# Unread identity products on TensorE in a two-layer decoder: first group's front and last group's FFN

## The chip, the cores and the metric

The kernel runs on one core of a Trainium2 chip. The metric is the device time in microseconds (us) of one execution, the median of several runs. TensorE multiplies at one of two clock levels, 1.2 or 2.4 GHz. The profile gives the level as the granted clock, a share of full speed (0.50 or 1.00; a mean of both where a stretch holds a change).

## What is computed

The reference passes x of shape (16, 128, 256) through two decoder layers, in float32:

```python
x = layernorm(x + L0_attn(x))          # causal attention, one head
x = layernorm(x + L0_xattn(x, ctx))    # 16 heads of 8 channels, causal convolution with k
x = layernorm(x + L0_ffn(x))           # ternary weights, quantised inputs
x = layernorm(x + L1_attn(x))          # linear recurrence with a decay
x = layernorm(x + L1_xattn(x, ctx))    # 16 query heads, 4 key heads of 128
x = layernorm(x + L1_ffn(x))           # fp8 gate and up, gelu, fp8 down
```

The 16 sequences are independent of each other until the end.

## The kernel before

Two sequences make a group, so there are eight groups. The work of a group goes through stations. Station "a" holds the front (`front`: layer 0's attention and its convolution) and, three groups later, the last FFN (`ffn`); "c" holds the ternary FFN and the recurrence; "q", "x", "y" and "o" hold the second cross attention; "s" is the set-up of the weights. Each engine has its own list of steps of these stations, interleaved by a written-out string of letters (`ORDER`), and runs it strictly in that order. Semaphores join the engines. PSUM has eight banks: A0 and A1 for station a, C0 and C1 for c, E0 and E1 for the scores, EQ for queries and keys, EY for the output product.

Before there is other work, TensorE has only the first group and the set-up: at the start it waits on VectorE, ScalarE and GpSimd between short bursts. At the end nothing is left but the last group's FFN: the last nine letters of TensorE's order are nine steps of station a.

The first group's front, in TensorE's order, with the lines of the profile:

- L972 scores (`a_sc`), then L978 transposes of the probabilities (`a_pT`), which wait for VectorE's normalised S0, then L983 `a_y`, which waits for ScalarE's copy PT0.
- L933 `abs_ps`, a sum for the ternary weights, which waits for ScalarE's L438 and so for a load of weights. VectorE makes the mean from it (L604 to L606), after it has written X of the front; ScalarE's two tanh (L443) wait for the mean, and stand in ScalarE's order ahead of its copy XTA (L477).
- L944 transposes X (`b_xT`), L991 `b_skip`, then eight convolution steps u0 to u7 (L1007, L1009, L1010), which wait for the products `prod` that VectorE and GpSimd make from XTA (L232). GpSimd's next products wait for u1.
- L1016 `b_oT`, then L1123, the first keys of the cross attention, which waits for the last load of the set-up, and L938, which waits for ScalarE's decay table.

The last group's FFN: L944 transposes X once the cross attention's norm is out (`ne_out`); L1037 makes the gate and up halves in four steps (`f_gf`), each of which waits until ScalarE and VectorE have emptied A0 and A1; then a table load and the gelu on ScalarE (L492), a product on VectorE (L719), L1044 transposes, ScalarE's copies A8T (L497), and L1051, the down product.

Of the kernel before, what the change touches and what calls it, by code (L numbers as in the profile page):

```python
# [6 lines left out]
P = 128  # L7
HALVES = DIM // P
GB = 2
GROUPS = BATCH // GB  # L10
# [5 lines left out]
XHEADS, XKV, XDIM = 16, 4, 128  # L16
# [9 lines left out]
def build_decoder(nc, a):  # L26
# [4 lines left out]
    with ctx:  # L31
        def sb(name, shape, dt=F):
            return ctx.enter_context(nc.sbuf_tensor(name, [P] + list(shape), dt))

        def sem(name):
            return ctx.enter_context(nc.semaphore(name))
# [16 lines left out]
        ident_bf = sb("ident_bf", [P], BF)  # L53
# [76 lines left out]
        A0, A1, C0, C1, E0, E1, EQ, EY = bank  # L130
        EB = (E0, E1)

        def rows(t):
            return t[:].rearrange("p (b d) -> p b d", b=GB)

        def cols(t):
            return t[:].rearrange("p (k r) -> p k r", k=HALVES)
# [7 lines left out]
        def seq(b):  # L145
            return slice(b * P, (b + 1) * P)
# [14 lines left out]
        sems = {n: sem(n) for n in names}  # L161

        def sig(ins, name):
            return ins.then_inc(sems[name], 1)

        def nth(g, per=1, j=0):

            return g * per + j + 1

        def settled(eng):  # L170
            eng.sem_inc(sems["passed"], 1)
# [19 lines left out]
        def a_free(eng, kind, g):  # L191

            if kind == "front" and g >= AHEAD:
                eng.wait_ge(sems["nf_out"], nth(g - AHEAD))
            elif kind == "front" and g > 0:
                eng.wait_ge(sems["na_out"], nth(g - 1, 3, 2))
            elif kind == "ffn":
                eng.wait_ge(sems["na_out"], nth(min(g + AHEAD - 1, GROUPS - 1), 3, 2))
                if g > GROUPS - AHEAD:
                    eng.wait_ge(sems["nf_out"], nth(g - 1))  # L200
# [702 lines left out]
        def _(pe):  # L903
# [37 lines left out]
            def transpose_rows(src, dst, name):  # L941
                for b in range(GB):
                    for k in range(HALVES):
                        ins = nc.tensor.transpose(cols(dst)[:, k, seq(b)], src[:, b, k * P:(k + 1) * P], ident[:])  # L944
                sig(ins, name)

            def project_rows(dst, xt, w, name):
                for b in range(GB):
                    for k in range(HALVES):
                        ins = nc.tensor.matmul(rows(dst)[:, b], xt(k, b), w(k), start=k == 0, stop=k == HALVES - 1)  # L950
                sig(ins, name)

            def front(g):
                x = X[g % XBUF]
                yield
                pe.wait_ge(sems["loaded_a"], 16 * for_group["a"])
                pe.wait_ge(sems["na_out"], nth(g, 3, 0))
                transpose_rows(Z, A0, "a_zT")
                yield
                pe.wait_ge(sems["a_xn"], nth(g))  # L960
                pe.wait_ge(sems["w_qk_in"], 1)
                for e in range(HALVES):
                    for k in range(HALVES):
                        ins = nc.tensor.matmul(cols(A1)[:, e], w_qk[:, k, e * P:(e + 1) * P], XTA[:, k], start=k == 0, stop=k == HALVES - 1)
                sig(ins, "a_qv")
                pe.wait_ge(sems["w_vo_in"], 1)
                project_rows(A0, lambda k, b: XTA[:, k, seq(b)], lambda k: w_vo[:, k], "a_qv")
                yield
                pe.wait_ge(sems["a_q"], nth(g))
                for b in range(GB):  # L970
                    for k in range(HALVES):
                        ins = nc.tensor.matmul(A1[:, seq(b)], QT[:, k, seq(b)], XTA[:, k, seq(b)], start=k == 0, stop=k == HALVES - 1)  # L972
                sig(ins, "a_sc")
                yield
                pe.wait_ge(sems["a_v"], nth(g))
                pe.wait_ge(sems["a_p"], nth(g))
                for b in range(GB):
                    ins = nc.tensor.transpose(A0[:, seq(b)], S0[:, seq(b)], ident[:])  # L978
                sig(ins, "a_pT")
                yield  # L980
                pe.wait_ge(sems["a_pTc"], nth(g))
                for b in range(GB):
                    ins = nc.tensor.matmul(rows(A1)[:, b], PT0[:, seq(b)], V[:, b], start=True, stop=True)  # L983
                sig(ins, "a_y")
                yield
                pe.wait_ge(sems["na_out"], nth(g, 3, 1))
                transpose_rows(x, A0, "b_xT")
                yield
                pe.wait_ge(sems["pool_const"], 2)
                pe.wait_ge(sems["b_w"], nth(g))  # L990
                sig(nc.tensor.matmul(A1[:], skip_w[:], SK[:].rearrange("p b d -> p (b d)"), start=True, stop=True), "b_skip")  # L991
                for u in range(8):
                    yield
                    hq, lb = u // 2, u % 2
                    if hq == 0:
                        pe.wait_ge(sems["b_kv0"], nth(g))
                    else:
                        pe.wait_ge(sems["b_kv"], nth(g, 3, hq - 1))
                    if u == 1:
                        pe.wait_ge(sems["b_skc"], nth(g))  # L1000
                    if u >= 2:
                        pe.wait_ge(sems["b_z"], nth(g, 8, u - 2))
                    out = (A0, A1)[u % 2][:].rearrange("p (b h n) -> p b h n", b=GB, h=4)
                    for h in range(4):
                        mv_ = prod[:, hq % 2, :, :, h * 64:(h + 1) * 64]
                        if lb == 0:
                            ins = nc.tensor.matmul(out[:, :, h], taps[:, hq * 4 + h, 0:P], mv_[:, 0], start=True, stop=True)  # L1007
                        else:
                            nc.tensor.matmul(out[:, :, h], taps[:, hq * 4 + h, 0:P], mv_[:, 1], start=True, stop=False)  # L1009
                            ins = nc.tensor.matmul(out[:, :, h], taps[:, hq * 4 + h, P:], mv_[:, 0], start=False, stop=True)  # L1010
                    sig(ins, "b_yps")
                yield
                pe.wait_ge(sems["b_ot"], nth(g))
                for b in range(GB):
                    for k in range(HALVES):
                        ins = nc.tensor.transpose(rows(A0)[:, b, k * P:(k + 1) * P], OT[:, k, b], ident[:])  # L1016
                sig(ins, "b_oT")

            def ffn(g):
                yield  # L1020
                a_free(pe, "ffn", g)
                pe.wait_ge(sems["ne_out"], nth(g))
                transpose_rows(X[g % XBUF], A0, "f_xT")
                for j in range(2 * GB):
                    yield
                    b, nh = j // 2, j % 2
                    if j == 0:
                        pe.wait_ge(sems["stage_used0"], 6)
                        pe.wait_ge(sems["stage_used1"], 6)
                    pe.wait_ge(sems["f_x8"], nth(g))  # L1030
                    if j >= 1:
                        pe.wait_ge(sems["f_g16"], nth(g, 2 * GB, j - 1))
                        pe.wait_ge(sems["f_f16"], nth(g, 2 * GB, j - 1))
                    settled(pe)
                    for k in range(2):
                        for h in range(HALVES):
                            ins = nc.tensor.matmul((A0, A1)[k][:], X8[:, h, seq(b)], w_gf[:, k, h, nh * BANK:(nh + 1) * BANK],  # L1037
                                                   start=h == 0, stop=h == HALVES - 1)
                    sig(ins, "f_gf")
                for b in range(GB):  # L1040
                    yield
                    pe.wait_ge(sems["f_a"], nth(g, GB, b))
                    for k in range(FFN_K):
                        ins = nc.tensor.transpose(as_bf((A0, A1)[b])[:, seq(k)], G16[:, b, seq(k)], ident_bf[:])  # L1044
                    sig(ins, "f_aT")
                for b in range(GB):
                    yield
                    pe.wait_ge(sems["f_a8"], nth(g, GB, b))
                    settled(pe)
                    for k in range(FFN_K):  # L1050
                        ins = nc.tensor.matmul((A0, A1)[b][:, 0:DIM], A8T[:, b, k], w_ln[:, k], start=k == 0, stop=k == FFN_K - 1)  # L1051
                    sig(ins, "f_y")
# [265 lines left out]
```

## Time and profile before

| | |
|---|---|
| median of 3 runs | 937.77 us (936.29 to 937.84) |
| profiled execution, its time | 936.48 us |
| its span, first to last instruction | 934.7 us |
| around the span | 1.8 us |
| mean granted clock of TensorE | 0.958 |
| TensorE busy | 829.3 us (89%) |
| VectorE busy | 714.5 us (76%) |
| ScalarE busy | 500.4 us (54%) |
| GpSimd busy | 263.0 us (28%) |

A busy share counts from an instruction's start to its modelled end; matmuls overlap, so it says when TensorE had work, not how fast it worked. The granted clock says that.

### The profile page before, as it was taken

The page shows a single profiled execution, that of the slowest core. Times are in us where ns is not written, and L with a number is a line of the kernel's source. Part 1 is how long each engine was busy: PE and PEld are TensorE (multiplying, and loading weights), DVE is VectorE, ACT ScalarE, POOL GpSimd, SP SyncE. Part 2 cuts the span into 40 slices and gives each one's busy share as a digit, 9 for nine tenths or more (in the row PEclk, how much of TensorE's full clock was granted, in tenths as well). Part 3 has the DMA queues.
Part 4 walks back from the last instruction along what each step waited for, and adds up shares of the span by engine and source line. Part 5 has one row for each costly group of instructions (what it writes and reads, how often), then busy time and mean ns, then how long its engine had stood idle before and what let it go on. Part 6 is the DMA issues. An engine that isn't in the chain of part 4 may idle for free.

```text
span 934.7 us, 14078 instructions
## 1 busy us (share of the span) xinstructions
PE 829.3 (89%) x4858; PEld 636.6 (68%) x4874; DVE 714.5 (76%) x1735; ACT 500.4 (54%) x1283; POOL 263.0 (28%) x298
## 2 busy tenths in 40 slices
PE   5654868998999999999999999998999999999964
PEld 4533746787686767976779768876779677767742
DVE  3587887878798889787988879688989696756443
ACT  3354116615544773368553587419552767577833
POOL 0323511343333133423134311442143311231100
PEclk9577989999999999999999999999999999999985
DMA  8861010000001000010000000010000000000000
GB/s 276 291 208 55 1 24 12 12 10 14 19 5 24 1 12 23 2 23 1 13 23 18 7 8 17 13 23 1 24 1 1 1 12 1 1 13 12 1 12 11
DMA packets 37062, 28.64 MB, mean 31 GB/s; under 512 B 18688, under 2 KB 34560, under 8 KB 36608
## 3 DMA queue, kind: packets, MB, share of 16 engines
q1 hardware_dynamic: 36992, 27.74, 9.8%
q8 instruction: 39, 0.64, 0.3%
q14 instruction: 31, 0.25, 0.1%
HBM read 25.64 MB, written 2.10 MB: 30 GB/s over the span
## 4 chain that ended last, share of the span: by engine, by line
PE 47%; DVE 34%; issue 10%; ACT 7%; POOL 1%; DMA 1%; SPq 1%; DVEq 0%; POOLq 0%; ACTq 0%
PE bank L1130 7%; PE bank L1226 6%; PE bank L950 5%; DVE S L879 4%; PE bank L1215 3%; PE bank L1205 3%; PE bank L1007 2%; PE bank L1123 2%; PE bank L1009 2%; PE bank L1010 2%; DVE amax L767 2%; PE bank L1037 2%; DVE H L766 2%; DVE mx L882 2%; DVE X L641 2%
## 5 line engine op out<-in xcount | busy, mean ns | idle before, releaser
L1130 PE MATMUL bank<-XTE,w_xq 128*128 128x256 f32 x512 | 126.1, 390 | 7.4 <-ACT QA L542 4.2
L575 ACT ACTIVATE S<-S,mx 128x128 f32<-128x128 f32 x256 | 99.4, 393 | 46.1 <-DVE mx L882 45.6
L1226 PE MATMUL bank<-w_xo,OX 128*128 128x256 f32 x512 | 116.2, 380 | 1.6 <-ACT OX L584 1.6
L1130 PEld LDWEIGHTS bank<-XTE,w_xq 128*128 128x128 f32 x512 | 96.5, 194 | 27.9 <-ACT QA L542 8.4
L1226 PEld LDWEIGHTS bank<-w_xo,OX 128*128 128x128 f32 x512 | 95.6, 190 | 18.2 <-issue 4.5
L541 ACT ACTIVATE QS<-bank,per_partition_sb 128x256 f32<-128x256 f32 x128 | 60.4, 472 | 80.9 <-PE bank L1130 80.8
L333 POOL TENSOR_TENSOR rq<-vq,minus_half 128x8 f32<-128x8 f32 x32 | 53.8, 1682 | 158.8 <-DVE vq L852 158.7
L879 DVE SCALAR_TENSOR_TENSOR S<-bank,rq,xmask 128x128 f32<-128x128 f32 x256 | 71.8, 343 | 15.4 <-PE bank L1205 10.5
L232 POOL TENSOR_TENSOR prod<-XTA,ccolA 128x256 f32<-128x256 f32 x96 | 63.0, 686 | 38.4 <-PE bank L1010 31.2
L1205 PEld LDWEIGHTS bank<-KTX,QA 128*128 128x128 f32 x512 | 63.5, 191 | 10.8 <-issue 9.3
L584 ACT ACTIVATE OX<-bank,bv_sb 128x512 f32<-128x512 f32 x64 | 43.6, 689 | 50.6 <-PE bank L1215 28.2
L1205 PE MATMUL bank<-KTX,QA 128*128 128x128 f32 x512 | 68.2, 278 | 0.7 <-ACT OX L584 0.6
L1215 PE MATMUL bank<-PT,VX 128*128 128x512 f32 x128 | 65.9, 606 | 1.8 <-ACT PT L579 1.7
L1123 PE MATMUL bank<-w_xkv_sb,ccolE 128*128 128x512 f32 x128 | 61.1, 600 | 1.0 <-DVE KX L857 0.9
L542 ACT ACTIVATE QA<-bank,per_partition_sb 128x256 f32<-128x256 f32 x128 | 60.7, 474 | 0.0
L1009 PE MATMUL bank<-prod,taps_sb 128*128 128x128 f32 x256 | 51.4, 283 | 1.2 <-DVE Zc L692 0.9
L579 ACT ACTIVATE PT<-bank 128x512 f32<-128x512 f32 x64 | 37.7, 600 | 26.5 <-PE bank L1210 26.4
L692 DVE TENSOR_TENSOR Zc<-bank,ccolA 128x512 f32<-128x512 f32 x64 | 43.7, 683 | 9.6 <-PE bank L1010 5.8
L1010 PE MATMUL bank<-prod,taps_sb 128*128 128x128 f32 x256 | 50.5, 280 | 0.0
L575 ACT ACTIVATION_READ_ACCUMULATOR S<-S,mx 128x1 f32 x256 | 48.9, 191 | 0.0
L886 DVE TENSOR_TENSOR S<-S,rs 128x512 f32<-128x512 f32 x64 | 46.3, 723 | 2.2
L1210 PE MATMUL bank<-ident,S 128*128 128x128 f32 x256 | 38.9, 277 | 9.0 <-DVE S L886 8.9
(222 smaller groups left out, 1780.8 us busy)
## 6 DMA issues: line engine op xcount, KB each, us to landing
xin<-in_x SPq DMA_DIRECT2D x8, 256.0 KB, 2.6
taps_sb<-in_taps SPq DMA_DIRECT2D x1, 2048.0 KB, 11.1
cnat<-in_ctx SPq DMA_DIRECT2D x8, 256.0 KB, 2.8
ccolA<-in_ctxT SPq DMA_DIRECT2D x32, 64.0 KB, 2.7
ccolE<-in_ctxT SPq DMA_DIRECT2D x16, 128.0 KB, 2.2
w_xq<-in_L_xattn_Wq SPq DMA_DIRECT2D x1, 2048.0 KB, 12.0
w_xo<-in_L_xattn_Wo SPq DMA_DIRECT2D x1, 2048.0 KB, 16.8
out_x<-X SPq DMA_DIRECT2D x8, 256.0 KB, 2.1
```

The lines of the kernel that those rows point to most:

```text
L232: ins = eng.tensor_tensor(prod[:, hq % 2, k, b].rearrange("p (h j i) -> p h j i", i=CONV_CH, j=CONV_CH), v.unsqueeze(2).broadcast_to([P, 4 ...
L541: nc.scalar.activation(QS[:, h], q, ACT.Square, bias=bq[:, hh:hh + 1])
L542: ins = nc.scalar.activation(QA[:, n % 2, h], q, ACT.Identity, bias=bq[:, hh:hh + 1])
L575: ins = nc.scalar.activation(S[:, b, seq(h)], S[:, b, seq(h)], ACT.Exp, bias=mx[:, b, h:h + 1], accum_out=sm[:, b, h:h + 1])
L879: ins = nc.vector.scalar_tensor_tensor(s3[:, h], EB[b][:, seq(h)], rq[:, n % 2, b * XGROUP + h:b * XGROUP + h + 1], xmask[:], ALU.mult, AL ...
L1009: nc.tensor.matmul(out[:, :, h], taps[:, hq * 4 + h, 0:P], mv_[:, 1], start=True, stop=False)
L1010: ins = nc.tensor.matmul(out[:, :, h], taps[:, hq * 4 + h, P:], mv_[:, 0], start=False, stop=True)
L1123: ins = nc.tensor.matmul(EQ[:], ccolE[:, k, b], w_xkv[:, k, v], start=k == 0, stop=k == HALVES - 1)
L1130: ins = nc.tensor.matmul(cols(EQ)[:, h], w_xq[:, k, hh * XDIM:(hh + 1) * XDIM], XTE[:, k], start=k == 0, stop=k == HALVES - 1)
L1205: ins = nc.tensor.matmul(EB[b][:, seq(h)], QA[:, n % 2, h, seq(b)], KTX[:, b, n], start=True, stop=True)
L1215: sig(nc.tensor.matmul(EB[b][:], VX[:, b, n * XDIM:(n + 1) * XDIM], PT[:, b], start=True, stop=True), f"e_o{b}")
L1226: ins = nc.tensor.matmul(rows(EY)[:, b], OX[:, h, b], w_xo[:, n * XGROUP + h], start=n == 0 and h == 0 and b == 0, stop=n == XKV - 1 and h ...
```

## The change

A helper issues n products of the bf16 identity with itself (128 by 128 by 128) into a bank that is free at the time. Nothing reads them, and they signal nothing. They stand behind the signalling instruction of a step, so no signal of the step itself is moved, and ahead of the next step's wait. In the first group there are 24, 30, 24 and 80 of them; in the last group's FFN 56 ahead of its first transposes, 10 after each of the first three `f_gf` steps and 50 after the fourth. Two waits are new on TensorE: for `pool_const` at 2 (GpSimd has made ident_bf and skip_w), and for the last `e_vq` (VectorE has read EQ for the last time).

```diff
+            def keep_clock(spare, n):
+
+                for _ in range(n):
+                    nc.tensor.matmul(spare[:, 0:P], ident_bf[:], ident_bf[:], start=True, stop=True)
@@ front, behind a_sc
+                if g == 0:
+                    pe.wait_ge(sems["pool_const"], 2)
+                    keep_clock(EY, 24)
@@ front, behind a_y
+                if g == 0:
+                    keep_clock(EY, 30)
@@ front, behind b_skip
+                if g == 0:
+                    keep_clock(EY, 24)
@@ front, behind b_oT
+                if g == 0:
+                    keep_clock(EY, 80)
@@ ffn
-                yield
+                last = g == GROUPS - 1
+                yield
+                if last:
+                    pe.wait_ge(sems["e_vq"], nth(g, XKV, XKV - 1))
+                    keep_clock(EQ, 56)
                 a_free(pe, "ffn", g)
@@ ffn, behind each f_gf
+                    if last:
+                        keep_clock(EQ, 10 if j < 2 * GB - 1 else 50)
```

TensorE's order in the first group's front before the change, from the score product to the first convolution step:

```order
L972 MATMUL bank<-XTA,QT 128x128 x4
L978 MATMUL bank<-ident,S 128x128 x2
L983 MATMUL bank<-V,PT 128x256 x2
L933 MATMUL bank<-abs_sum,ones 128x1 x2
L944 MATMUL bank<-ident,X 128x128 x4
L991 MATMUL bank<-SK,skip_w 128x512
L1007 MATMUL bank<-prod,taps_sb 128x2x64 x4
```

The same place on TensorE in the changed kernel, whose lines are numbered higher:

```order
L977 MATMUL bank<-XTA,QT 128x128 x4
L956 MATMUL bank<-ident_bf 128x128 x24
L986 MATMUL bank<-ident,S 128x128 x2
L991 MATMUL bank<-V,PT 128x256 x2
L956 MATMUL bank<-ident_bf 128x128 x30
L933 MATMUL bank<-abs_sum,ones 128x1 x2
L944 MATMUL bank<-ident,X 128x128 x4
L1001 MATMUL bank<-SK,skip_w 128x512
L956 MATMUL bank<-ident_bf 128x128 x24
L1019 MATMUL bank<-prod,taps_sb 128x2x64 x4
```

No instruction has changed its place among the others; the runs of L956 stand between them.

TensorE's order at the end of the program before the change, from the last output product on:

```order
L1226 MATMUL bank<-w_xo,OX 128x256 x8
L944 MATMUL bank<-ident,X 128x128 x4
L1037 MATMUL bank<-w_gf,X 128x512 x16
L1044 MATMUL bank<-ident_bf,G 128x128 x16
L1051 MATMUL bank<-w_ln,A8T 128x256 x16
```

And in the changed kernel:

```order
L1246 MATMUL bank<-w_xo,OX 128x256 x8
L956 MATMUL bank<-ident_bf 128x128 x56
L944 MATMUL bank<-ident,X 128x128 x4
L1055 MATMUL bank<-w_gf,X 128x512 x4
L956 MATMUL bank<-ident_bf 128x128 x10
L1055 MATMUL bank<-w_gf,X 128x512 x4
L956 MATMUL bank<-ident_bf 128x128 x10
L1055 MATMUL bank<-w_gf,X 128x512 x4
L956 MATMUL bank<-ident_bf 128x128 x10
L1055 MATMUL bank<-w_gf,X 128x512 x4
L956 MATMUL bank<-ident_bf 128x128 x50
L1064 MATMUL bank<-ident_bf,G 128x128 x16
```

The run of 16 gate and up products is cut in four, with the new products in each cut and at both ends.

## Rows read from the trace of the kernel before

**Rows 1.** The page: granted clock in 40 equal slices of the span, in tenths

```profile
PEclk9577989999999999999999999999999999999985
```

**Rows 2.** Windows of the front: stretch and length, busy per engine, PEclk, DMA, GB/s

```profile
20.50:22.00 1.50, 0.00 (x0) 0.00 (x0) 1.45 (x3) 1.50 (x2) 0.00 (x0) 1.00 0.93 178
22.00:23.00 1.00, 0.00 (x0) 0.00 (x0) 0.69 (x1) 1.00 (x5) 0.00 (x0) 0.76 0.24 37
37.20:42.80 5.60, 5.54 (x26) 5.54 (x27) 2.00 (x5) 2.12 (x4) 0.00 (x0) 0.50 1.06 357
42.80:52.00 9.20, 8.99 (x76) 8.61 (x75) 8.49 (x13) 0.00 (x0) 5.98 (x9) 0.99 1.03 395
```

**Rows 3.** Timeline of the first front: start, length, engine, line, [idle before <- releaser]

```profile
23.86 0.66 PE L978 MATMUL bank<-ident,S 128*128 128x128 f32 x2 [3.38 <-DVE S L667]
24.99 2.07 PE L983 MATMUL bank<-V,PT 128*128 128x256 f32 x4 [0.47 <-ACT PT L474]
...
28.69 0.98 PE L933 MATMUL bank<-abs_sum,ones 128*128 128x1 f32 x4 [1.63 <-ACT w_gv L438]
...
31.24 2.19 ACT L443 ACTIVATE stage<-stage,inv_mean 128x1024 f32<-128x1024 f32 x2 [2.69 <-DVE inv_mean L606]
...
37.26 2.08 PE L1007 MATMUL bank<-prod,taps_sb 128*128 128x128 f32 x8 [2.98 <-DVE prod L232]
...
42.55 1.28 PE L1007 MATMUL bank<-prod,taps_sb 128*128 128x128 f32 x8
...
60.37 0.69 PE L938 MATMUL bank<-ident,dscale 128*128 128x128 f32 x2 [4.43 <-ACT dscale L452]
```

**Rows 4.** Timeline: the same kinds of work at a granted clock of 1.00

```profile
45.49 1.06 PE L1007 MATMUL bank<-prod,taps_sb 128*128 128x128 f32 x8
...
48.38 1.06 PE L1007 MATMUL bank<-prod,taps_sb 128*128 128x128 f32 x8
...
78.62 0.38 PE L978 MATMUL bank<-ident,S 128*128 128x128 f32 x2
...
79.83 1.13 PE L983 MATMUL bank<-V,PT 128*128 128x256 f32 x4 [0.83 <-ACT PT L474]
```

**Rows 5.** Timeline and window of a later fall of the clock

```profile
223.36 0.66 PE L1210 MATMUL bank<-ident,S 128*128 128x128 f32 x4 [1.41 <-DVE S L886]
...
223.00:225.00 2.00, 1.64 (x7) 1.46 (x8) 1.97 (x4) 1.67 (x4) 2.00 (x2) 0.73 0.00 0
```

**Rows 6.** Window of the end in which the clock falls

```profile
906.00:907.00 1.00, 0.17 (x1) 0.20 (x2) 0.68 (x2) 0.00 (x0) 0.00 (x0) 0.79 0.02 8
```

**Rows 7.** Timeline of the last group's FFN

```profile
899.33 3.69 PE L1226 MATMUL bank<-w_xo,OX 128*128 128x256 f32 x16 [0.87 <-ACT OX L584]
...
906.83 1.09 PE L944 MATMUL bank<-ident,X 128*128 128x128 f32 x4 [3.80 <-DVE X L641]
...
908.89 1.87 PE L1037 MATMUL bank<-w_gf,X 128*128 128x512 fp8e4 x4 [0.97 <-ACT X L483]
...
911.74 1.86 PE L1037 MATMUL bank<-w_gf,X 128*128 128x512 fp8e4 x4 [0.98 <-DVE F L714]
...
923.15 1.98 PE L1044 MATMUL bank<-ident_bf,G 128*128 128x128 bf16 x16 [3.85 <-DVE G L719]
...
924.31 1.98 ACT L497 ACTIVATE A8T<-bank 128x1024 fp8e4<-128x1024 bf16 x2 [1.06 <-PE bank L1044]
...
925.48 2.66 PE L1051 MATMUL bank<-w_ln,A8T 128*128 128x256 fp8e4 x16 [0.34 <-ACT A8T L497]
```

**Rows 8.** Timeline: the last FFN's kinds of work at a granted clock of 1.00

```profile
106.84 0.60 PE L944 MATMUL bank<-ident,X 128*128 128x128 f32 x4
...
297.88 1.03 PE L1037 MATMUL bank<-w_gf,X 128*128 128x512 fp8e4 x4
...
313.69 1.10 PE L1044 MATMUL bank<-ident_bf,G 128*128 128x128 bf16 x16
...
316.25 1.91 PE L1051 MATMUL bank<-w_ln,A8T 128*128 128x256 fp8e4 x16
```

## The prediction

> **What bounds the kernel now.** I read the page's slices of the granted clock first, since the new products can only act through it. TensorE runs at 2.4 GHz for nearly the whole span; the slices below 9 lie among the first six (0 to 140 us) and are the last two (from 888 us) [rows 1]. In between TensorE always has work, and nothing is added there. So the change has two places, and they share nothing but the length of the program: what the first front wins is passed on by the fixed orders, since every later step waits for data, and what the last FFN wins is won outright.
>
> In the windows of the front the reader is to see the clock fall between 22 and 23 us (1.00, then a mean of 0.76, so near 22.5) and come back only near 43 us [rows 2]. TensorE had been idle since 23.86 - 3.38 = 20.48 us [rows 3]: the fall came 2.0 us into the wait. The timeline then gives what ran at 1.2 GHz, and what it waited for. At the end the clock falls between 906 and 907 us (0.79, near 906.6) [rows 6], 3.5 us after the output product's end at 903.02 [rows 7], and the whole last FFN runs at half speed: nothing else is left in the kernel, and each piece of it waits for the one before. Its steps are the chain, TensorE's share included.
>
> **What is added.** The new products are bf16, 128 by 128, the form of L1044, whose 16 take 1.10 us at full clock [rows 8]; with the last one's drain off that is about 0.06 us each, and 0.11 at half clock (the 16 there take 1.98 with a pause inside [rows 7]). At full clock the runs last: 24, 1.4 us; 30, 1.8; 80, 4.8; 56, 3.4; 10, 0.6; 50, 3.0. Their covers are the waits they stand in: 3.38 us ahead of L978 for the first 24, 1.63 ahead of L933 for the 30 (more if `a_y` ends earlier), 2.98 ahead of L1007 for the second 24 [rows 3], 3.80 for the 56, 0.98 for each 10, 3.85 for the 50 [rows 7]. The 80 delay L1123, the keys, and with it L938, which waited 4.43 us for ScalarE's table [rows 3]; 4.8 leaves 0.4 us over, and L938's result is not wanted by the next steps, so I cost them at 0, up to 0.4. The two added waits are for signals long given: 0. At full clock, then, the additions cost nothing; at half clock the 56 take 6.2 us (2.4 over their cover), the 50 take 5.5 (1.6 over), each 10 takes 1.1 (0.1 over), the 30 take 3.3.
>
> **The last FFN.** If the clock stays up, from the rows of the same work at full clock [rows 7, 8]:
> - L944, 1.09 to 0.60: 0.49 us.
> - L1037, 1.87 to 1.03, four times, since each step waits for the emptying of the one before: 4 x 0.84 = 3.36 us.
> - L1044 and L1051: before, 925.48 + 2.66 - 923.15 = 4.99 us. After: the first eight transposes take 0.55 plus the 0.13 to ScalarE instead of 1.16; ScalarE's two copies stay 1.98 and now set the pace; then 0.15 to TensorE and the second down product, half of 1.91. That is 0.68 + 1.98 + 0.15 + 0.96 = 3.77, so 1.2 us less; I take 1.05, since the halves share one drain.
>
> Sum 4.9 us. Does it stay up? The new idle stretches are 3.80 - 3.4 = 0.4 us, about 1.0 ahead of the first L1037, 0.4 in each step, 0.9 ahead of L1044. Falls in this trace came 2.0 and 3.5 us into a wait, or after two waits close together: at 223.9 us, the second of them 1.41 us long with a short transpose ahead of it [rows 5]. The two stretches around L944 add up to 1.4 us; that is less, and I take the clock to stay. If it falls there after all, one or two of the four steps are slow before the now dense stream brings it back: 1.7 to 2.2 us lost.
>
> **The first front.** Two gains, one behind the other:
> - L978 and L983 at full clock: 0.66 to 0.38 and 2.07 to 1.13 [rows 3, 4], 1.2 us. X and the mean follow `a_y`; L933 could hold the mean back, since its input comes by DMA at 28.69, but at 0.5 us long it is done at 29.2, ahead of the mean's other input. So the tanh starts at 31.24 - 1.15 = 30.1, and XTA and the products after it.
> - u0 and u1 at full clock: from L1007 to L1007, 42.55 - 37.26 = 5.29 us before [rows 3], 48.38 - 45.49 = 2.89 at full clock [rows 4]: 2.4 us. GpSimd's next products wait for u1, and the rest of the convolution was at full clock already, so this moves on whole.
>
> Both ends: nothing (the clock falls as early as before), or 3.55 us. Which, hangs on the two waits that the 24s fill only in part: 3.4 - 1.4 = 2.0 us ahead of L978, and after `b_skip` 2.98 + about 1.0 (its end is earlier than u0 moves) - 1.4, some 2.6 us ahead of u0. Both lie between the 1.41 that on its own is kept and the 3.38 that is not, and a fall came exactly 2.0 us into a wait. I give each an even chance or a little less, so one of the two gains in part: 1.3 us, range 0 to 3.55.
>
> To this the Trainium skill has a rule ("TensorE: Matmul & The Clock Gate", "HAM oscillation"): only a long idle gap between bursts throttles the clock again, shorter ones are harmless. By it all new gaps would be kept, and the front would win its whole 3.55 us. The trace does not quite agree: its fall near 22.5 us came 2.0 us into the gap, and the one near 223.9 with gaps of 1.41 us. I keep it as a rival.
>
> **The sum** is made against the profiled execution, 936.48 us (span 934.7, 1.8 around it): 936.48 - 4.9 - 1.3 = 930.3. The shown median is 1.3 us above that execution, and the three runs span 1.55 us; where the clock changes sides is not tied to the program's start, and I take it that this makes that spread. I add 0.4 for it: **930.7 us**.
>
> **The rivals.**
> - *The front keeps its clock too.* 936.48 - 4.9 - 3.55 = 928.0, with the spread 928.4. For it: no gap left is as long as any of the trace's single waits that lost the clock. Against it: the 2.0 us at 22.5. 16%.
> - *The end loses its clock once, or the front wins nothing.* 930.7 + 1.3 = 932.0 to 930.7 + 2.2 = 932.9; both together 934.2. For it: 1.4 us in two pieces near L944 is not far from the pieces that lost it at 223.9. 16%.
> - *Slower: the identity products do not count as activity.* Then the clock falls as before, and the runs behind it last twice as long. Place: the last FFN, 50 products at 5.5 us against 3.85, +1.6; three times 10 at +0.1; in the front the 30 push L933 from 28.69 to 30.4, and the mean by 0.2. The 56 are through before the fall. Sum +2.1: 936.48 + 2.1 = 938.6, with the spread 939.0; if the clock has fallen ahead of the 56 as well, their 2.4 over makes it 941.4. It decides from the point where the 50 outlast 3.85 us, 0.077 us a product. For it: they multiply almost only zeros, and no row shows such a product. Against it: the stream that brought the clock back near 927 began with 16 products that have the identity as one operand, L1044 [rows 7]. 5%.
> - *The change does nothing:* the clock falls in the leftover gaps all the same and returns sooner by as much as the overshoots cost. Near 936.5. 3%.
>
> On the third the Trainium skill speaks against this change ("TensorE: Matmul & The Clock Gate", "Part 4: PE-mode transpose"): transposes by an identity do not count as busy in the same way. The new ones are plain products, so the rule does not strictly hold for them; applied to them it would give that rival's result.
>
> **How the numbers follow.** The forecast has 60%, the rivals 16, 16, 5 and 3. A measurement of this kernel tells about 0.2%, 1.9 us, from no change. Faster by more (below 935.9): the forecast and the first two rivals, 92%. Same, 6%: the last rival, and three parts in five of the slow one, whose 939.0 lies inside the bound. Slower by more (above 939.6): the slow one with the 56 paid too, 2%. The likeliest case alone spans 929.3 to 932.0. The range to hold 8 in 10 takes in the front's full gain at one end and the end's loss of one fall at the other: 928.2 to 933.4.
>
> **What would show it.** The last FFN at a granted clock of 1.00 from 903 us on, L1037's four at about 1.03 us and 2.0 us apart, down from 2.85; L1044 still waiting for VectorE, not for the 50. In the front: L983 near 1.1 us and the tanh near 30.1 if the first 24 hold the clock; L1007's first eight near 1.1 us and u1 done near 39 us if the second do. The prediction is wrong if L1037 stays at 1.87, if a run of L956 ends after the data its successor waits for, or if the early gain is lost again in the first group's next waits on the way to 130 us, where the clock falls and rises too.

## The result, and the profile after

The changed kernel takes 930.78 us (median of 6 runs, 929.26 to 932.53), the kernel before, timed beside it, 937.36 (6 runs, 935.77 to 938.31): a ratio of 0.9932, 95% interval 0.9917 to 0.9947. The forecast was 930.7.

The page of the changed kernel, the granted clock in 40 slices, beside which [rows 1] is to be laid. Its profiled execution is the slowest of the six, 932.53 us, span 930.6.

```profile
PEclk9787889999999999999999999999999999999999
```

The last two slices have gone from 8 and 5 to 9 and 9; among the first five, 9 5 7 7 9 has become 9 7 8 7 8. The timeline of the last FFN, with start, length, engine, line and the idle time ahead, answers to [rows 7]:

```profile
903.72 3.29 PE L956 MATMUL bank<-ident_bf 128*128 128x128 bf16 x56
...
907.68 0.63 PE L944 MATMUL bank<-ident,X 128*128 128x128 f32 x4 [0.68 <-DVE X L641]
...
909.29 1.02 PE L1055 MATMUL bank<-w_gf,X 128*128 128x512 fp8e4 x4 [0.97 <-ACT X L483]
...
910.15 0.72 PE L956 MATMUL bank<-ident_bf 128*128 128x128 bf16 x10
...
911.29 1.02 PE L1055 MATMUL bank<-w_gf,X 128*128 128x512 fp8e4 x4 [0.42 <-DVE F L714]
...
916.16 2.96 PE L956 MATMUL bank<-ident_bf 128*128 128x128 bf16 x50
...
920.18 0.62 PE L1064 MATMUL bank<-ident_bf,G 128*128 128x128 bf16 x8 [1.06 <-DVE G L719]
...
922.09 1.98 PE L1071 MATMUL bank<-w_ln,A8T 128*128 128x256 fp8e4 x16 [0.34 <-ACT A8T L497]
```

Everything is there that the prediction named: gate steps 1.02 us long and 2.00 apart, no successor that waits for a run of L956, and an idle 0.68 us ahead of L944 that does not lose the clock. From the output product's end to the end of the span it is 903.88 to 930.6, 26.7 us, against 903.02 to 934.7, 31.7 us, before [rows 7].

The first front, to be read against [rows 3]:

```profile
20.54 1.50 PE L956 MATMUL bank<-ident_bf 128*128 128x128 bf16 x24
24.08 0.41 PE L986 MATMUL bank<-ident,S 128*128 128x128 f32 x2 [2.04 <-DVE S L667]
24.96 1.13 PE L991 MATMUL bank<-V,PT 128*128 128x256 f32 x4 [0.47 <-ACT PT L474]
25.93 1.84 PE L956 MATMUL bank<-ident_bf 128*128 128x128 bf16 x30
30.24 0.89 PE L933 MATMUL bank<-abs_sum,ones 128*128 128x1 f32 x4 [2.47 <-ACT w_gv L438]
...
33.59 1.59 PE L956 MATMUL bank<-ident_bf 128*128 128x128 bf16 x24
37.77 2.08 PE L1019 MATMUL bank<-prod,taps_sb 128*128 128x128 f32 x8 [2.59 <-DVE prod L232]
...
43.05 1.51 PE L1019 MATMUL bank<-prod,taps_sb 128*128 128x128 f32 x8
```

L991 runs at full clock, 1.13 us. But then L933 waits for L438 until 30.24, where it waited until 28.69 before, and u0 starts at 37.77, half a microsecond later than before. The clock was lost twice on the way, ahead of L933 and again ahead of u0; a mean granted clock of 1.00, then 0.68, and later 0.50 (the value behind the five busy times, fields as in [rows 2]):

```profile
27.00:30.00 3.00, 0.77 (x14) 0.59 (x11) 1.76 (x7) 1.08 (x3) 0.86 (x2) 1.00 0.95 327
30.00:31.00 1.00, 0.76 (x5) 0.79 (x5) 0.00 (x0) 0.10 (x2) 1.00 (x1) 0.68 0.89 318
...
37.20:38.00 0.80, 0.23 (x1) 0.23 (x2) 0.80 (x2) 0.46 (x1) 0.24 (x1) 0.50 0.97 326
```

ScalarE's rows in the same execution say why L933 waited:

```profile
28.95 1.06 ACT L438 ACTIVATE w_gv<-stage 128x1024 bf16<-128x1024 f32 x1 [1.92 <-DMA stage<-in_w2T]
...
31.75 2.19 ACT L443 ACTIVATE stage<-stage,inv_mean 128x1024 f32<-128x1024 f32 x2 [1.65 <-DVE inv_mean L606]
```

L438 could start on the second half of w2T, a load, at 28.95 us; in the profile before it could at 27.39. u0 and u1 took 43.05 - 37.77 = 5.28 us, at half clock. So this one execution wins 4.9 us at the end and nothing in the front (the last output product ends 0.9 us later than before). It is the slowest of the six, and if the front gained, it was in the five faster ones.

### The profile page after: what moved, and what is told of

Same layout as the page of the kernel before. It is cut to its first block, busy times and chain, and to the rows that moved or that the text cites. A ratio compares the mean times of both kernels' runs of the same rounds, so it can differ in the third digit from the quotient of the medians.

```text
span 930.6 us, 14666 instructions
## 1 busy us (share of the span) xinstructions
PE 839.5 (90%) x5152; PEld 653.0 (70%) x5168; DVE 714.6 (77%) x1735; ACT 500.6 (54%) x1283; POOL 263.0 (28%) x298
## 2 busy tenths in 40 slices
DMA packets 37065, 28.69 MB, mean 31 GB/s; under 512 B 18688, under 2 KB 34560, under 8 KB 36608
## 4 chain that ended last, share of the span: by engine, by line
PE 48%; DVE 34%; issue 8%; ACT 7%; POOL 1%; DMA 1%; SPq 0%; DVEq 0%; POOLq 0%; ACTq 0%
PE bank L1150 7%; PE bank L1246 6%; PE bank L950 5%; DVE S L879 4%; PE bank L1235 3%; PE bank L1225 3%; PE bank L1019 3%; PE bank L1143 2%; PE bank L1021 2%; PE bank L1022 2%; DVE amax L767 2%; PE bank L1055 2%; DVE H L766 2%; DVE mx L882 2%; DVE X L641 2%
## 5 line engine op out<-in xcount | busy, mean ns | idle before, releaser
L232 POOL TENSOR_TENSOR prod<-XTA,ccolA 128x256 f32<-128x256 f32 x96 | 63.0, 687 | 40.1 <-PE bank L1022 31.4
L584 ACT ACTIVATE OX<-bank,bv_sb 128x512 f32<-128x512 f32 x64 | 43.6, 689 | 50.6 <-PE bank L1235 28.2
L1235 PE MATMUL bank<-PT,VX 128*128 128x512 f32 x128 | 66.1, 607 | 1.8 <-ACT PT L579 1.7
L579 ACT ACTIVATE PT<-bank 128x512 f32<-128x512 f32 x64 | 37.6, 600 | 26.5 <-PE bank L1230 26.4
## 6 DMA issues: line engine op xcount, KB each, us to landing
w_xq<-in_L_xattn_Wq SPq DMA_DIRECT2D x1, 2048.0 KB, 12.5
```

Source lines behind the costliest of these rows:

```text
L232: ins = eng.tensor_tensor(prod[:, hq % 2, k, b].rearrange("p (h j i) -> p h j i", i=CONV_CH, j=CONV_CH), v.unsqueeze(2).broadcast_to([P, 4 ...
L1235: sig(nc.tensor.matmul(EB[b][:], VX[:, b, n * XDIM:(n + 1) * XDIM], PT[:, b], start=True, stop=True), f"e_o{b}")
```

## Experiments

Each was timed in five rounds beside the kernel before (medians 937.12 to 937.40). Since one profile is one execution, the table below gives, for each profile, the moments on which the reading rests, from the rows of its timeline: when the first group's score product (L972 before) starts, which is ahead of every product of the change; when ScalarE's L438 had the second half of w2T; u0, the first convolution step; u0 to u2, the two steps that the prediction priced at 5.29 or 2.89; from the first group's first queries (`w_xq`) to the end of the last output product; and from there to the end. The profiled execution is the fastest of its kernel for e2 and e12 and the slowest for the change, e3, e6 and e10, so these columns show where time went in one execution and are no means.

| kernel | median us | ratio (95%) | scores | w2T | u0 | u0 to u2 | queries to output | end |
|---|---|---|---|---|---|---|---|---|
| before | 937.36 | 1 | 19.3 | 27.4 | 37.3 | 5.29 | 771.8 | 31.7 |
| the change | 930.78 | 0.9932 (0.9917, 0.9947) | 19.6 | 28.9 | 37.8 | 5.28 | 771.8 | 26.7 |
| e1 end only | 931.63 | 0.9944 (0.9931, 0.9958) | 19.7 | 28.3 | 37.6 | 5.28 | 771.7 | 26.7 |
| e2 front only | 935.93 | 0.9986 (0.9973, 0.9999) | 18.3 | 27.5 | 36.0 | 2.78 | 771.4 | 31.4 |
| e3 without the 80 | 931.18 | 0.9935 (0.9921, 0.9949) | 19.8 | 30.4 | 39.3 | 2.78 | 773.2 | 26.7 |
| e4 as transposes | 932.53 | 0.9951 (0.9935, 0.9968) | 20.0 | 31.2 | 40.1 | 4.41 | 771.5 | 26.7 |
| e5 only the 56 | 934.03 | 0.9971 (0.9958, 0.9983) | 19.2 | 29.1 | 38.0 | 5.19 | 771.9 | 28.0 |
| e6 100 for the 50 | 933.90 | 0.9966 (0.9955, 0.9978) | 20.2 | 29.6 | 38.5 | 4.22 | 773.3 | 28.3 |
| e7 longer front | 928.35 | 0.9910 (0.9898, 0.9923) | 18.9 | 27.9 | 36.4 | 2.78 | 771.4 | 26.7 |
| e8 and three gaps | 927.96 | 0.9909 (0.9895, 0.9922) | 19.2 | 28.9 | 37.5 | 2.78 | 771.2 | 26.7 |
| e9 before, loads d later | 936.48 | 0.9991 (0.9981, 1.0002) | 19.0 | 27.1 | 37.0 | 5.29 | 771.9 | 31.6 |
| e10 change, loads d later | 931.11 | 0.9932 (0.9916, 0.9948) | 19.4 | 28.1 | 36.6 | 4.26 | 773.4 | 26.7 |
| e11 e8, loads d later | 929.41 | 0.9920 (0.9906, 0.9935) | 20.0 | 28.2 | 36.7 | 2.78 | 771.1 | 26.7 |
| e12 e7 and one gap | 927.30 | 0.9899 (0.9881, 0.9916) | 18.3 | 27.2 | 35.7 | 2.78 | 769.2 | 26.7 |

**e1, the end only.**

```diff
-                if g == 0:
-                    pe.wait_ge(sems["pool_const"], 2)
-                    keep_clock(EY, 24)
...
-                if g == 0:
-                    keep_clock(EY, 80)
```

> Only the products of the last group's FFN (56, 10, 10, 10, 50) are kept; the four runs of the first front are gone. Theory: the two places are independent, and the end wins 4.9 us in every execution, since no wait there is left long enough to lose the clock: 932.2 to 932.8 us against 937.4, ratio 0.995, with L1055's four at 1.02 us each and 2.0 us apart. Rival (most of the gain is the front's, the end is one lucky execution): 935 us or more, and a profile in which the clock falls within the last FFN.

The end alone wins 0.56%, 5.2 us by the ratio where 4.9 was expected, and its own stretch is 26.7 us, as in every profile that has all of the end's products. The rival falls.

**e2, the front only.**

```diff
-                last = g == GROUPS - 1
+                last = False
```

> Only the first front's 24, 30, 24 and 80 are kept; the last FFN is as before. Theory: the front wins 0 to 3.55 us, 1.3 on the mean, by which of its waits loses the clock and by when the second weight load lands: 935.5 to 936.5 us, ratio near 0.9985, and the single executions lie further apart than those of the other kernels. Rival (the front keeps its clock in nearly every execution): 934 us, ratio 0.9965. Rival (the runs in the front are only a cost, since the load of w2T or the tanh holds it): 937.4 or more.

0.14%, 1.3 us (the interval reaches from 0.1 to 2.5), and the 12 executions reach from 931.6 to 938.64, where the 17 of before beside them reach from 935.12 to 939.67. The profiled one is the fastest, 931.6. About 1 us of that is none of the change's: its score product starts at 18.3 us, ahead of every new product, where the profile before has 19.3. In it the clock fell near 24.3 us, while L991 ran, behind the wait that the first 24 had left, and rose during the 30; the second 24 and both convolution steps had all of it: 2.78 us from L1019 to L1019 instead of 5.29:

```profile
25.00 3.12 PE L956 MATMUL bank<-ident_bf 128*128 128x128 bf16 x30
28.75 0.58 PE L933 MATMUL bank<-abs_sum,ones 128*128 128x1 f32 x4 [0.63 <-ACT w_gv L438]
...
31.32 1.50 PE L956 MATMUL bank<-ident_bf 128*128 128x128 bf16 x24
35.97 1.16 PE L1019 MATMUL bank<-prod,taps_sb 128*128 128x128 f32 x8 [3.15 <-DVE prod L232]
```

The 30 took 3.12 us, most of them at half clock: behind them L933 still waited 0.63 us, so even that cost nothing. Ahead of u0 there is a wait of 3.15 us that did not lose the clock, where 2.59 did in the change. By the ratios the two parts together give 5.2 + 1.3 = 6.5 us, and the whole change 6.4 (0.68%).

**e3, without the 80.**

```diff
-                if g == 0:
-                    keep_clock(EY, 80)
```

> The whole change without the 80 products behind b_oT. Theory: they win nothing, because the wait ahead of the ternary FFN's first transposes is 4.9 us long and loses the clock with them or without them, and they cost nothing, because the keys behind them are not wanted for 10 us: the time of the whole change, 930.8 us within 1 us. Rival (they hold the clock over the set-up's last steps): 1 to 2 us slower, 932 to 933, with the transposes and gate products near 66 to 71 us slower than in the whole change.

931.18 against 930.78, ratios 0.9935 and 0.9932 with intervals that nearly coincide. From `b_oT` to the ternary FFN's first transposes it is 52.77 to 65.24 here and 53.97 to 66.45 with the 80, 12.5 us both times.

**e4, the same products as transposes.**

```diff
-                    nc.tensor.matmul(spare[:, 0:P], ident_bf[:], ident_bf[:], start=True, stop=True)
+                    nc.tensor.transpose(as_bf(spare)[:, 0:P], ident_bf[:], ident_bf[:])
```

> Each new product is issued as a transpose of the identity (the same operands, the same count, the output in bf16), to see whether a transpose counts as activity. Theory: it does, since the stream that brought the clock back near 927 us before the change was half transposes: 930.8 us within 1.5, and a clock of 1.00 through the last FFN. Rival (a transpose by an identity does not count): the clock falls near 907 us, the 50 last 5.5 us against a wait of 3.85, and the time is 938 to 939.

```profile
904.46 3.29 PE L956 MATMUL bank<-ident_bf 128*128 128x128 bf16 x56
908.42 0.63 PE L944 MATMUL bank<-ident,X 128*128 128x128 f32 x4 [0.67 <-DVE X L641]
...
910.02 1.02 PE L1055 MATMUL bank<-w_gf,X 128*128 128x512 fp8e4 x4 [0.97 <-ACT X L483]
```

Transposes hold the clock through the last FFN as the products do, to the hundredth of a microsecond, and the end takes 26.7 us. The median lies 1.75 us above the change's, a little outside the 1.5 that I gave; the intervals overlap, and in the profiled execution u0 starts at 40.1 us against 37.8, since w2T came at 31.2 us. Whether more of it is the transposes' is open. The Trainium skill's sentence that transposes do not count as busy in the same way ("TensorE: Matmul & The Clock Gate", "Part 4: PE-mode transpose") is not borne out by this profile: at the end 56 and 50 transposes in the place of the products left the granted clock at 1.00.

**e5, only the 56.** Against e1, from which it takes the 10s and the 50 too:

```diff
-                    if last:
-                        keep_clock(EQ, 10 if j < 2 * GB - 1 else 50)
```

> Of the end's products only the 56 ahead of L944 are kept; the 10s, the 50 and the front's are gone. Theory: the 56 carry the clock over the 3.8 us wait, and the four gate steps keep it up by themselves or lose it on the way, since their waits are 1.0 us long between 1.0 us of work; then the 3.85 us wait for the gelu loses it, and L1064 and L1071 run at half. From the output product's end to the program's end: 28 us if the steps keep the clock (26.7 + 1.1 for the last two pieces), 30 to 31 if they lose it at once; time 933 to 935.5. Rival (the 10s are what holds it, and the 56 only delay the fall): 31 us and 936.5.

28.0 us in the profile, the number given for steps that keep the clock by themselves:

```profile
910.85 1.02 PE L1046 MATMUL bank<-w_gf,X 128*128 128x512 fp8e4 x4 [0.98 <-DVE F L714]
...
919.88 1.98 PE L1053 MATMUL bank<-ident_bf,G 128*128 128x128 bf16 x16 [3.85 <-DVE G L719]
...
922.21 2.65 PE L1060 MATMUL bank<-w_ln,A8T 128*128 128x256 fp8e4 x16 [0.34 <-ACT A8T L497]
```

But the eleven executions reach from 932.4 to 936.85 and their median is 2.4 us above e1's, where this profile's end is 1.3 above. I take it that in some of them the steps lose the clock; no profile shows one, but the mean granted clock of the whole execution, which is measured for each, is 0.958 and 0.960 in the two slowest (936.85 and 936.82 us) and 0.967 in the three fastest. So the 56 alone bring about half of the end's gain (2.7 us by the ratio, of e1's 5.2), and the 10s and the 50 bring the rest.

**e6, 100 for the 50.** Against e1:

```diff
-                        keep_clock(EQ, 10 if j < 2 * GB - 1 else 50)
+                        keep_clock(EQ, 10 if j < 2 * GB - 1 else 100)
```

> The end's products only, with 100 instead of 50 behind the fourth gate step. Theory: a run costs nothing as long as it ends before the data its successor waits for, and beyond that what it is over: 100 products last 2.96 - 0.2 + 50 x 0.056 = 5.6 us against a wait of 3.85, so 1.6 to 1.8 us more than with the 50: 933.3 us against 931.6, and L1064 waits for nothing. Rival (TensorE takes unread products aside, or the wait has more room): 931.6.

```profile
917.79 5.75 PE L956 MATMUL bank<-ident_bf 128*128 128x128 bf16 x100
923.37 1.06 PE L1055 MATMUL bank<-ident_bf,G 128*128 128x128 bf16 x16
```

L1055, the transposes of this kernel, has no wait left and starts in the run's drain. The end takes 28.25 us against e1's 26.73, 1.5 more than with the 50, close to the 1.6 to 1.8 expected. The median is 2.3 above e1's. A run costs what it is over its cover (the wait that it stands in).

**e7, the front's runs lengthened; e8, three more gaps.**

```diff
-                    keep_clock(EY, 24)
+                    keep_clock(EY, 48)
...
-                    keep_clock(EY, 30)
+                    keep_clock(EY, 46)
...
-                    keep_clock(EY, 24)
+                    keep_clock(EY, 52)
@@ e8 alone: ahead of c_qx, of the first c_q3, and of e_xT
+                if g == 0:
+                    keep_clock(EY, 76)
...
+                    if g == 0 and b == 0:
+                        keep_clock(EY, 140)
...
+                if g == 0:
+                    keep_clock(EY, 68)
```

> The whole change, with the front's runs lengthened to fill their waits: 24 to 48 behind a_sc, 30 to 46 behind a_y, 24 to 52 behind b_skip. Theory: then no wait of the front loses the clock, except where the load of w2T lands very late, and the convolution's first two steps run at full clock in nearly every execution: 2.4 us x the half of the executions that lost it, 1 us faster than the whole change: 929.7. The first term (1.15 us) stays mostly unpaid, since the mean waits for the load. Rival (the front's gain is held by the load alone): 930.8, no change, and u2 begins at the same time as in the change.

e7 is 2.4 us faster than the change, where 1 us was expected (intervals 0.9898 to 0.9923 and 0.9917 to 0.9947 overlap at the edge, so the size is uncertain), and its four executions lie within 0.8 us, 928.24 to 929.01, against 3.3 for the change's six. Its rows:

```profile
29.16 0.58 PE L933 MATMUL bank<-abs_sum,ones 128*128 128x1 f32 x4 [1.13 <-ACT w_gv L438]
31.58 3.07 PE L956 MATMUL bank<-ident_bf 128*128 128x128 bf16 x52
36.38 1.16 PE L1019 MATMUL bank<-prod,taps_sb 128*128 128x128 f32 x8 [1.74 <-DVE prod L232]
39.16 1.06 PE L1019 MATMUL bank<-prod,taps_sb 128*128 128x128 f32 x8
```

The two profiled executions differ by 4.2 us. Of these, 2.5 lie in u0 and u1, 0.6 ahead of the score product and 0.8 between that and u0. The gain is passed on: u2 starts 3.9 us earlier, the first queries 3.7, and the last output product ends 4.1 us earlier.

> As the one before, with three more runs in the first group: 76 ahead of the ternary FFN's first transposes (a wait of 4.9 us), 140 ahead of the transposes of its hidden half (8.6 us), 68 ahead of the cross attention's transposes (4.45 us). Theory: the clock falls at 64, 85 and 129 us and the bursts behind these waits run at half; kept up they win about 1.5, 1.3 and 1.9 us, of which most lies on the way: 4 us less, 925.5 to 926.5. Rival (these bursts lie beside VectorE's work, which is busy nine tenths there, and the gain is swallowed within the dense middle): 929 or more.

e8 is 0.4 us below e7, where I expected 4. That cannot be told from none, and so goes the rival's way, although the time lies under its 929. The page of e8 has a 9 in every slice but one (an 8), so the products did their work:

```profile
PEclk9999899999999999999999999999999999999999
```

From the ternary FFN's first transposes to the first queries it takes 128.21 - 63.39 = 64.8 us against 128.39 - 62.32 = 66.1 in e7, and w2T one microsecond later took most of that away again. But e12, with the 68 alone, has 64.9 there, and profiles with none of the three runs lie between 65.1 and 66.7: no profile shows a gain of the 76 and the 140.

**e9, e10, e11, the loads of group d later.**

```diff
                 stage_load(1, "w2T")
-                load("d", w_rkv[:], by_k(a["w_rkv"]))
-                load("d", w_o1[:], by_k(a["w_o1"]))
-                load("d", upto[:], a["upto"])
                 yield
                 stage_load(2, "w3T")
+                load("d", w_rkv[:], by_k(a["w_rkv"]))
+                load("d", w_o1[:], by_k(a["w_o1"]))
+                load("d", upto[:], a["upto"])
```

> The kernel before, with nothing changed but the set-up's loads of group d (w_rkv, w_o1, upto), which are issued behind w3T's loads instead of right behind w2T's. Theory: the second half of w2T lands between 27.4 and 31.2 us in the profiles so far because it shares the DMA engines with w_rkv; moved away it lands about 2 us earlier and hardly varies. The kernel before gains little from it, since its mean waits for X at 30.7 us unless the load lands past 29: 0 to 1 us, 936.5. Rival (w2T is late because of what was issued ahead of it, the ctx loads): the landing is as before, and so is the time, 937.3.

> The whole change, with the same move of the loads of group d. Theory: in the changed kernel the mean waits for w2T and not for X, so an early landing frees the first term of the front, 1.15 us, and the wait ahead of L933 gets short enough to keep the clock: 1.2 to 2.5 us less than the change, 928.3 to 929.6. Rival (the front's spread is that of the clock's moments alone): 930.8 with the same spread of 3.3 us.

> All gaps of the first group filled, the longer runs of the front, and the loads of group d moved. Theory: the parts add up, since one fixes the landing of w2T and the others the clock: 1 us below the one with all gaps filled, 926.9, and single executions within 1 us. Rival (with the clock kept the load no longer matters, or the moved loads delay w3T and the last loads): 928 or more.

With w_rkv out of the way the landing is 27.1, 28.1 and 28.2 us; with it behind w2T the profiles of this study had 27.2 to 31.2. Part of that range is the moment of issue, which moves with the score product (2.7 us behind its start in every profile). From the issue of w2T to L438's start it took 5.4 to 8.5 us in the eleven profiles with w_rkv right behind, and 5.4, 6.0 and 5.5 us in e9, e10 and e11. Three profiles cannot prove it, but none is late. e9 came out as expected (0.1%, not distinguishable from none). e10 did not: 931.11, no faster than the change, as its rival said. Its profiled execution, the slowest of six, has the tanh early, at 30.59, and loses that twice: the clock falls ahead of u0 after all (3.03 us of wait, and 4.26 us for the two steps), and it returns at 142 us instead of 136, so that the stretch from the queries on takes 773.4 us instead of 771.8. e11's median, 929.41 where 926.9 was expected, is 1.45 us above e8's (the intervals overlap), and its profile shows a cost that e8 has not:

```profile
57.84 3.63 PE L1147 MATMUL bank<-w_xkv_sb,ccolE 128*128 128x512 f32 x4 [2.52 <-DMA w_xo<-in_L_xattn_Wo]
...
61.52 4.41 PE L956 MATMUL bank<-ident_bf 128*128 128x128 bf16 x76
65.76 0.61 PE L1084 MATMUL bank<-ident_bf,QQ 128*128 128x128 bf16 x8
```

The last load lands later, the keys wait for it and run at half clock, and the 76 behind them are then over their cover: VectorE had QQ at 62.6 us, L1084 starts at 65.76. A run that is safe behind one wait is not safe behind another that can move.

**e12, e7 and one gap.** e7 with the 68 ahead of the cross attention's transposes.

> The front's longer runs (48, 46, 52, 80), the end's, and one more run: 68 ahead of the cross attention's first transposes, where the clock fell near 129 us and rose at 135 us in most profiles, at 141 to 143 in three. Theory: those three executions lost 1.5 us between the first queries and the last output product (773.3 us against 771.3 to 771.8), and the burst of the others ran at half as well; with the 68 that stretch takes 770.5 to 771.3 in every execution: 927.5 us, spread under 1 us, against 928.35 without them. Rival (the run is over its cover, or the gain is swallowed by the dense middle): 928.3 or more, and a stretch of 771.4 or more.

927.30, the fastest median; but its four executions reach from 924.22 to 928.82, so the spread did not close, and it is not separated from e7 or e8. The profiled one is the fastest, and 4.1 us below e7's; its score product starts 0.6 us earlier, also ahead of every new product. The stretch from the queries on took 769.2 us, less than I had given. Windows around the same work, a pair of score transposes and the queries behind it, with length, busy time per engine and granted clock, first the change, then e12, which is 6 us ahead there:

```profile
223.00:226.00 3.00, 1.79 (x8) 1.58 (x9) 2.90 (x8) 2.52 (x8) 2.52 (x3) 0.82 0.00 0
```

```profile
218.00:221.00 3.00, 3.00 (x15) 2.31 (x16) 2.93 (x6) 1.89 (x5) 1.58 (x2) 1.00 0.00 0
```

In the change, as before [rows 5], the clock falls near 225 us; in e12 it does not. e8 has the 68 too, and it takes 771.2 us with a fall:

```profile
218.00:221.00 3.00, 1.59 (x9) 1.20 (x8) 2.75 (x9) 2.93 (x10) 2.20 (x3) 0.88 0.00 0
221.00:223.00 2.00, 2.00 (x7) 1.53 (x6) 1.93 (x5) 0.00 (x0) 0.33 (x1) 0.50 0.01 4
```

That one fall goes with 2.0 us, and 1.7 of them lie right there: from the transposes after which the clock falls to the score products behind the queries it is 219.62 to 226.35, 6.73 us, in e8 and 217.88 to 222.92, 5.04 us, in e12. Both kernels have the 68, so that run does not decide whether the clock falls there; and e11, which has it too, shows no fall there: what decides it is open.

## Why the prediction was right, point by point

**The end, 4.9 us.** Right in sum and in its terms. L944 took 0.63 us (0.60 forecast), L1037 1.02 each (1.03), L1044 and L1051 with the wait between them 3.89 (3.94), and the end's stretch went from 31.66 to 26.74 us in the profiles. The clock stayed up through the two waits near L944 in all nine profiles of after and of the experiments that have all of the end's products, and in e5's and e6's, and e1 measured 5.2 us alone. The prediction's 1.41 us wait "that on its own is kept" is in none of its rows; the trace before has a kept wait of that size elsewhere, 1.48 us ahead of L1016 at 53.27.

**The additions, 0.** Right: at full clock 24, 30, 80, 56, 10 and 50 lasted 1.50, 1.84, 4.63, 3.29, 0.72 and 2.96 us with their drain, and none was over its cover. e6 confirms the price of being over.

**The front, 1.3 us.** The size was met (e2: 1.3, interval 0.1 to 2.5), but the way there was right only in part. The two leftover waits were as long as forecast: 2.04 us ahead of L986 (2.0) and 2.59 ahead of u0 (2.6). The second term, u0 and u1, is as priced: 5.28 or 2.78 us, by whether the clock is kept, with values between. The first, 1.15 us through an earlier tanh, rested on L933's input landing at 28.69 in every execution. That step failed: with the clock kept the mean waits for the load and not for X, and L438 had the load between 8.1 and 11.2 us behind the start of the score product. In e11, where it came 8.2 behind (8.1 before), the tanh did come early, 10.7 us behind the score product against 11.9. In the change's profile it came 9.4 behind, and the tanh 12.2. The late load also made a third wait, 2.47 us ahead of L933, in which the profile lost the clock and which the prediction had not counted. u0 starts 8.5 us behind L438's start at full clock (36.38 - 27.87 in e7, 35.69 - 27.16 in e12), where before, at half clock, the mean waited for X and u0 started at 37.3 even with the landing at 27.4.

**The spread and the 0.4 us.** I laid the 1.55 us between the runs of before to the clock's moments alone. The profiles show three sources. One is the start of the score product, 18.3 to 20.2 us: TensorE's first instruction starts between 7.8 and 8.9 us, when a load has landed, and the eight products of L918 behind it take from 1.89 us (e2) to 3.15 (e6), by when the clock first rises. No run puts products there. The second is w2T, 5.4 to 8.5 us from its issue. The third are later moments of the clock: u0 at half; 1.5 us when it returned at 141 to 143 instead of 135 us; 2.0 near 220. The sum stood on a profiled execution 0.9 us under the median of six (936.48 against 937.36); its 6.2 us taken from that median give 931.2, and the measured 930.78 lies 0.4 us below. That the stated 930.7 came out to a tenth was luck.

**The rivals.** By the Trainium skill's rule ("TensorE: Matmul & The Clock Gate", "HAM oscillation") the front would have kept its clock, and the prediction gave that rival 928.4. The change did lose the clock in its profile after a wait of 2.47 us ahead of L933 and again after 2.59 ahead of u0, while 3.15 us in e2 was kept; so length alone does not decide. The rival's time was reached only with the waits filled, in e7 (928.35). The slow rival, that identity products do not count, fell at once, and for transposes too. Losing the clock once at the end did not occur in any profile that has all of the end's products.

## What to carry to other kernels

Where a latency chain at one end of a kernel leaves TensorE idle between small bursts, count what the bursts would take at full clock, and fill the waits with unread products that end just before the data comes: 136 of them in the last FFN, at some 0.06 us each (2.96 for 50), cost nothing here and won 5 us. Size each run by the shortest wait it can meet, and put none behind a step whose own start can move, as a load's landing. And read the spread of single executions: a gain that depends on whether a half-filled wait keeps the clock is a reason to fill the wait wholly. Here that brought another 2.4 us in the median; e7's four executions agreed within 0.8 us, though e12's four, with the same front, lay 4.6 apart. Before crediting a fast execution to a change, look at a moment ahead of the change: the score product alone moved by 2 us.

## What the runs showed of the hardware

The time from the issue of one load of 0.5 MB to its use on ScalarE varied between executions by 3 us (5.4 to 8.5 us, in the eleven profiles with w_rkv's load right behind it); on the clock of the program it was 27.2 to 31.2 us, and in the four profiles in which the front is wholly as before (before, e1, e5, e6) 27.4, 28.3, 29.1 and 29.6. Identity times identity keeps the clock, as product and as transpose alike. A wait of 3.15 us at full clock was kept once and waits of 2.47 and 2.59 were not; all three stood between bursts of one or two microseconds.
